# Shifted-token layers on one Trainium2 core: who scales and shifts the feed-forward norm's tiles, VectorE or ScalarE

## What is computed

```python
def shift_tokens(t):
    a, s = jnp.split(t, 2, -1)
    s = jnp.pad(s, ((0, 0), (1, 0), (0, 0)))[:, :-1]
    return jnp.concatenate([a, s], -1)
def ffn_layer(x, g, bln, W1, b1, W2, b2):
    mu = x.mean(-1, keepdims=True)
    var = ((x - mu) ** 2).mean(-1, keepdims=True)
    xn = (x - mu) / jnp.sqrt(var + 1e-05) * g + bln
    hg = xn @ W1 + b1
    a, gate = jnp.split(hg, 2, -1)
    return a * jax.nn.gelu(gate, approximate=False) @ W2 + b2
for i in range(6):
    x = attn_layer(shift_tokens(x), Wqkv[i], q_scale[i], k_scale[i], Wo[i]) + x
    x = ffn_layer(shift_tokens(x), ln_g[i], ln_b[i], W1[i], b1[i], W2[i], b2[i]) + x
```

## Time and profile before

| what | value |
|---|---|
| median of 3 runs | 4652.31 us (4650.04 to 4658.37) |
| profiled execution, its own time | 4656.79 us |
| its span | 4655.0 us |
| PE busy | 4112.3 us (88%) |
| PE weight loads | 2362.1 us (51%) |
| DVE busy | 3561.9 us (77%) |
| ACT busy | 2988.6 us (64%) |
| POOL busy | 2212.4 us (48%) |
| granted TensorE clock, mean | 0.935 |

### The profile page before, as it was taken

The page is one execution under the profiler, slowest core; times in us unless marked ns, Lnnn a source line. Parts: engine busy times, 40 slices in busy tenths (PEclk is TensorE's granted clock), DMA queues, the critical chain, the costliest instruction groups (busy, mean ns, idle before and its releaser), DMA issues. The chain is left out here.

```text
span 4655.0 us, 112822 instructions
## 1 busy us (share of the span) xinstructions
PE 4112.3 (88%) x40172; PEld 2362.1 (51%) x40175; DVE 3561.9 (77%) x8496; ACT 2988.6 (64%) x5496; POOL 2212.4 (48%) x1392
## 2 busy tenths in 40 slices
PE   8969999999999999999999999999999953747635
PEld 5644555555555555555555555555555532635533
DVE  7878888888888888888888888888888846356441
ACT  3427777777777777777777777777777745645302
POOL 0006665665656656566566656656565500140006
PEclk9989999999999999999999999999999975868557
DMA  1013222322223222232222322223222200000202
GB/s 41 1 54 67 62 58 62 80 59 61 60 60 81 63 59 60 58 82 65 59 59 60 76 65 63 57 64 75 64 60 61 58 17 12 1 1 6 82 9 35
DMA packets 187828, 246.44 MB, mean 53 GB/s; under 512 B 88677, under 2 KB 129383, under 8 KB 187367
## 3 DMA queue, kind: packets, MB, share of 16 engines
q1 hardware_dynamic: 182054, 240.47, 22.2%
q0 software_dynamic: 5632, 4.33, 0.7%
HBM read 41.65 MB, written 14.30 MB: 12 GB/s over the span
## 5 line engine op out<-in xcount | busy, mean ns | idle before, releaser
L1234 POOL TENSOR_TENSOR f_rot_a<-f_rot_a,f_norm 128x1024 f32<-128x1024 f32 x384 | 730.4, 1902 | 996.1 <-DVE f_norm L1073 963.6
L1226 POOL TENSOR_TENSOR f_rot_a<-f_rot_a,f_rot_b 128x1024 f32<-128x1024 f32 x384 | 908.5, 2366 | 246.3 <-issue 213.6
L832 PE MATMUL f_bank<-f_w_vo,f_xs_t 128*64 128x512 f32 x3072 | 828.5, 617 | 24.5 <-ACT f_vo L1303 24.5
L1303 ACT ACTIVATE f_vo<-f_bank 128x512 f32<-128x512 f32 x768 | 457.0, 595 | 395.9 <-PE f_bank L832 385.9
L1294 ACT ACTIVATE f_squares<-f_bank 128x512 f32<-128x512 f32 x768 | 456.4, 594 | 295.5 <-PE f_bank L819 215.6
L1052 DVE TENSOR_TENSOR f_rot_a<-f_bank,f_rot 128x512 f32<-128x512 f32 x768 | 525.0, 684 | 83.4 <-DVE f_stat L1101 42.3
L1055 DVE TENSOR_TENSOR f_rot_b<-f_bank,f_rot 128x512 f32<-128x512 f32 x768 | 516.8, 673 | 0.0
L864 PEld LDWEIGHTS f_bank<-f_k_t,f_q_t 128*32 128x32 f32 x12288 | 313.6, 109 | 315.4 <-issue 162.4
L1059 DVE TENSOR_REDUCE f_sums<-f_squares 128x16 f32<-128x1024 f32 x384 | 464.9, 1211 | 1.6
L1315 ACT ACTIVATE f_k_t<-f_bank 64x512 f32<-64x512 f32 x768 | 449.2, 585 | 4.8 <-PE f_bank L854 0.3
L1240 POOL TENSOR_TENSOR f_prob<-f_score,f_stat 128x512 f32<-128x512 f32 x384 | 400.4, 1043 | 98.6 <-DVE f_stat L1105 98.6
(11 more groups left out here) (445 smaller groups left out, 7235.4 us busy)
## 6 DMA issues: line engine op xcount, KB each, us to landing
f_vo_off<-f_vo SPq DMA_DIRECT2D x1152, 128.0 KB, 2.3
f_vo_off<-f_vo SPq DMA_DIRECT2D x384, 64.0 KB, 2.0
f_w_qk<-in_Wqk SPq DMA_DIRECT2D x12, 512.0 KB, 5.9
f_vo_dram<-f_vo_pair SPq DMA_DIRECT2D x48, 128.0 KB, 1.8
f_x_shifted<-s_all SPq DMA_DIRECT2D x48, 128.0 KB
f_x_shifted<-s_all SPq DMA_DIRECT2D x48, 127.0 KB
f_w_vo<-f_vo_dram SPq DMA_DIRECT2D x10, 512.0 KB, 4.0
e_w<-in_e_W SPq DMA_DIRECT2D x2, 2048.0 KB, 12.1
```

The lines of the kernel that those rows point to most:

```text
L832: done = nc.tensor.matmul(bank[V][64 * n:64 * n + 64, :], x, w_vo[:, 4 * g:4 * g + 4, n, :], start=True, stop=True)
L1226: nc.gpsimd.tensor_tensor(rot_a[:, slot, :, :], rot_a[:, slot, :, :], rot_b[:, g, :, :], ALU.add).then_inc(rot_summed, 1)
L1234: nc.gpsimd.tensor_tensor(heads, heads, over(norm[:, 16 * g:16 * g + 16], [128, 16, HEAD_DIM]), ALU.mult).then_inc(qk_normed, 1)
L1303: nc.scalar.activation(vo[:, g, 2 * (t % 2) + j, :], flat(V), ACT.Copy).then_inc((va_copied, vb_copied)[j], 1)
```

## The change: what it does

VectorE no longer writes the normalised tiles. In its place in round 1 it makes one instruction, four columns `-mean * inverse deviation` (`offsets`), and signals `f_measured`. ScalarE then makes the four tiles as `x * scale + bias` with the Identity function, in two pairs: tiles 0 and 1 between the square of q's first half and `copy_k` of the first half, tiles 2 and 3 between the square of k's second half and `copy_q` of the second half. `f_normed` comes from the last of the four. Nothing is changed on PE, POOL and SP.

```diff
+        f_offset = sb("f_offset", [128, PASS_TILES])
...
-            def normalise(p):
+            def offsets(p):
                 if live(p + 2, 0):
                     dve.wait_ge(norms_made, count(p + 2, 1))
                 else:
                     chain.wait()
                 if has(p, 1):
-                    dve.wait_ge(f_turned, p)
-                for t in range(PASS_TILES):
-                    last = nc.vector.tensor_scalar(f_n[:, 128 * t:128 * t + 128], x_shifted[:, t, :], f_mv[:, t, 0:1], norm[:, 32 + t:33 + t], ALU.subtract, ALU.mult)
-                    if t < PASS_TILES - 1:
-                        chain.mark(last)
-                last.then_inc(f_normed, 1)
+                    dve.wait_ge(f_normed, p + 1)
+                nc.vector.scalar_tensor_tensor(f_offset[:, :], f_mv[:, :, 0], -1.0, norm[:, 32:32 + PASS_TILES], ALU.mult, ALU.mult).then_inc(f_measured, 1)
...
                     if r == 1 and has(p, 2):
-                        normalise(p - 2)
+                        offsets(p - 2)
...
+            def normalise(p, half):
+                act.wait_ge(f_measured, p + 1)
+                if half == 0 and has(p, 1):
+                    act.wait_ge(f_turned, p)
+                for t in (2 * half, 2 * half + 1):
+                    last = nc.scalar.activation(f_n[:, 128 * t:128 * t + 128], x_shifted[:, t, :], ACT.Identity, bias=f_offset[:, t:t + 1], scale=norm[:, 32 + t:33 + t])
+                if half == 1:
+                    last.then_inc(f_normed, 1)
...
                     if on(r):
                         square(p, r, 0, 0)
+                    if r == 1 and has(p, 2):
+                        normalise(p - 2, 0)
                     if on(r - 1):
                         copy_k(p, r - 1, 0)
                         seed(p, r - 1, 0)
                         copy_values(p, r - 1, 1, 1)
                     if on(r):
                         square(p, r, 1, 1)
+                    if r == 1 and has(p, 2):
+                        normalise(p - 2, 1)
```

More of the change, by code:

```diff
@@ L575, in shifted_layers @@
         f_gate, gate_in, f_gelu, f_up = sem("f_gate"), sem("gate_in"), sem("f_gelu"), sem("f_up")
-        f_hidden, f_done, x_stored = sem("f_hidden"), sem("f_done"), sem("x_stored")
+        f_hidden, f_done, x_stored, f_measured = sem("f_hidden"), sem("f_done"), sem("x_stored"), sem("f_measured")
         ctx.callback(clear, nc, used)
```

## The result

The changed kernel takes 4688.65 us (median of 4 runs, 4685.7 to 4693.1) against 4653.63 us of the kernel before on the same chip: ratio 1.0075 [1.0058, 1.0093]. It is slower by 35.0 us where 34.5 were forecast. The profiled execution took 4685.7 us by its own time, with a span of 4683.9 us. The lines of the changed file are not those of the file before: `scores` is L865 (before L864), the turned norm L911 (L910), the turn of k L855 (L854), the projection of k L820 (L819), ACT's square L1292 (L1294), `copy_k` L1313 (L1315), `seed` L1319 (L1321), DVE's rotation L1053 (L1052), `length` L1060 (L1059), `store` L1145 (L1147). The columns are L1132, the Identity instructions L1341.

The account below looks back on a forecast made before the run. PE was taken to bound the kernel, with ACT lacking slack before `scores`. 46 passes x 0.77 = 35.4 us, less 0.9, gave +34.5 and 4687 us (+0.74%); own range 4676 to 4695, 8-in-10 range 4651 to 4702.

Parts of the forecast that it names:

- What bounds the kernel: PE, busy 976.4 of 1000 us; in round 1 ACT has at most 0.23 us of slack before `scores`.
- 1, the relief of DVE: Round 1: DVE gains 3.1 us a pass but then waits for ACT's square of k; worth 0.
- The estimate that DVE's busy time falls by 150 us: Expected sign in the profile after: DVE busy some 150 us less, ACT 92 us more.
- 2, the first pair: Two Identity instructions on ACT before `copy_k` in round 1 delay PE by 0.77 us a pass.
- The estimate that stands beside the sum: Skill page's formula for ACT's small tiles: 0.29 us each, 0.59 the pair, 27 us over 46 passes.
- 3, the second pair: Two Identity instructions between the square of k and `copy_q` fill 0.77 of ACT's 0.83 us idle time; cost 0.
- 4, the waits: ACT's wait for `f_measured` costs 0: DVE signals three us before ACT comes; later signals cost nothing either.
- 5, the ends: Tail norms taken at 0, at most 0.6 us each; pass 2 loses PE's 0.91 us wait for DVE once.
- The sum: 46 live passes x 0.77 = 35.4 us, less 0.9: +34.5 us.
- DVE was the bound: Faster: round 1's wait for the store closes, 0.33 us a pass, giving 4636 us; chance 0.14.
- Both partly: No change: half the pair hides, 0.38 us paid, and the store wait closes, -0.33; 4654 us; chance 0.12.
- ACT becomes the bound in more places: Slower still: a pair takes 1.05 us with a wait in front of each, 4700 us; chance 0.09.

Follow-up runs that it names:

- e4: Kernel before, norm still on DVE, plus two spare Identity instructions on ACT in front of `copy_k` in round 1, waiting for nothing: ratio 1.0070.
- e1: Changed kernel with all four Identity instructions behind ACT's square of k, none in front of `copy_k`: ratio 0.9997 against the kernel before.
- e3: Kernel before without the four normalising instructions on any engine; DVE makes only the columns and signals with them: ratio 0.9994.
- e9: Changed kernel with all four Identity instructions behind ACT's exponential and the columns made on DVE at the end of round 0: 0.9998 against the kernel before.
- e2: Changed kernel with three Identity instructions in front of `copy_k` and one behind ACT's square of k: ratio 1.0113 against the kernel before.
- e5: Changed kernel with columns first in DVE's round 1 and all four Identity instructions right after ACT's exponential: ratio 1.0025 against the kernel before.
- e7: Kernel before with only the store of pass p-3 moved on DVE to right behind the four normalising instructions: ratio 0.9960.

## Why the prediction was right, point by point

- **What bounds the kernel.** Right. PE is the bound at 97.6%, and ACT has no slack in front of `seed`: shown by e4, where two spare instructions there cost 0.70%, and e1, where their absence costs nothing.
- **1, the relief of DVE, taken at 0.** Right: e3 and e9. The price of the columns inside this step, 0.16 us, was wrong by a factor of ten: 1.73 us measured. It did no harm in passes 3 to 47, because even so they end at 2052.31, 1.3 us before ACT asks for them at 2053.63. In pass 2 it did (see 5). The estimate that DVE's busy time falls by 150 us failed by it: it fell by 3561.9 - 3490.4 = 71.5 us. ACT's rose by 3061.2 - 2988.6 = 72.6 us and not by 92, because instructions that overlap are counted once: 96 pairs x 0.77 = 74.
- **2, the first pair, 0.77 us on the path.** Right, and in the split foreseen: 0.69 at `scores`, the tenth of slack there lost again at L911 (0.09). Over the 44 intervals behind pass 3 the mean is 0.74. The third instruction of e2 confirms the price by itself. The spacing taken from the next block held: two take 0.87, so one starts 0.385 after the other. The estimate that stands beside the sum, 0.29 us for each and 27 us in all, was too low by a quarter.
- **3, the second pair, taken at 0.** Right. More: e1 shows that all four would fit there, since the turned norm's wait for the store covers what is late.
- **4, the waits, taken at 0.** Right for passes 3 to 47, by a margin of 1.3 us that e5, with another order, did not have.
- **5, the ends.** Incomplete. In pass 2 PE's wait of 0.91 us goes, as forecast, but a longer one comes. There is no down projection in that pass, so ACT comes to its first pair earlier by the 2.8 us that it takes elsewhere, ahead of the columns, and `scores` waits for it. The columns begin there at 479.89; at the forecast 0.16 us they would have been ready before ACT needed them (481.65 - 1.28 = 480.37), at 1.73 they are not:

```profile
481.65 0.88 ACT L1341 ACTIVATE f_f_n<-f_x_shifted,f_f_offset,f_norm 128x128 f32<-128x128 f32 x2 [1.28 <-DVE f_f_offset L1132]
```

```profile
484.24 1.08 PE L865 MATMUL f_bank<-f_k_t,f_q_t 128*32 128x128 f32 x32 [2.00 <-ACT f_bank L1319]
```

From the projection of k in front of `scores` to the turned norm, pass 2 takes 487.48 - 481.11 = 6.37 us against 485.63 - 480.19 = 5.44: 0.93 slower, where +0.77 - 0.91 = -0.14 was forecast. Right behind it a wait of 0.85 us goes that the forecast did not name, at the next `scores`, before and after:

```profile
489.10 1.08 PE L864 MATMUL f_bank<-f_k_t,f_q_t 128*32 128x128 f32 x32 [0.85 <-ACT f_bank L1321]
```

```profile
490.03 1.08 PE L865 MATMUL f_bank<-f_k_t,f_q_t 128*32 128x128 f32 x32
```

The delay against the kernel before falls there from 1.85 to 0.93 us, so the stretch from the norm of pass 2 to this point costs nothing in all, by two errors that cancel.

- **The sum.** +34.5 forecast, +35.0 measured. Some of the closeness is chance. From the first norm to the turned norm of pass 47 the profile has 34.3 - 0.92 = 33.4 us, 1.1 under the forecast: 0.74 a pass in place of 0.77. To these come the 0.92 us lost before the first norm, for which no cause is shown, and 0.9 us between pass 47 and the last turned norm in the tail (3790.55 - 3703.66 against 3755.32 - 3669.33). For the tail 0 was forecast, and e4, which has its norm on DVE, shows the same 0.9. That makes 35.2 us. Yet the profiled spans differ by only 28.9, since the blocks behind this one, which nobody changed, took some 6 us less in that execution. The interval of the ratio stands for +27 to +43 us.
- **The rival "DVE was the bound"** had a true part: the wait for the store is real, 0.33 us a pass. But what holds the store is its place in DVE's order behind ACT's square of k, not the amount of work on DVE: moving it wins the time (e7), relieving DVE does not (e3, e9).
- **The other two rivals** are answered by the timelines. "Both partly" needed a pair that hides by half and a store that comes early: of the 0.77 us 0.69 stand at `scores` and 0.09 at L911, which still waits for the store. "ACT becomes the bound in more places" needed 1.05 us for a pair and a wait in front of each: a pair takes 0.77 us from its start to the start of what follows, and in the pass shown ACT is not idle in front of either.

## What to carry to other kernels

Before work is moved from a busy engine to a less busy one, look at the row behind the place where it lands: an engine idle 26% of the time can have no slack at that place, and there each instruction costs its full length in every pass, while the same instructions a few places further down its list cost nothing. When the relieved engine's next instruction already coincides with the end of another engine's work, its relief only becomes a wait. And a wait that names an engine may be a matter of that engine's order: here moving one instruction up, with nothing offloaded, gave 0.4%.

## What the runs showed of the hardware

One DVE instruction of 128 x 4 took 0.15 us with POOL idle (e9), 0.91 (e5) and 1.73 us (changed kernel) beside POOL. The POOL rows of the changed kernel and of e5 show why:

```profile
2050.38 1.90 POOL L1232 TENSOR_TENSOR f_rot_a<-f_rot_a,f_norm 128x1024 f32<-128x1024 f32 x1 [0.17 <-POOL f_rot_a L1224]
```

```profile
2038.55 2.36 POOL L1224 TENSOR_TENSOR f_rot_a<-f_rot_a,f_rot_b 128x1024 f32<-128x1024 f32 x1 [0.40 <-issue]
```

POOL's instruction ends at 2052.28 and DVE's at 2052.31; in e5 at 2040.91 and 2040.93. So DVE's small instruction, whose two inputs lie in SBUF, is held until the running POOL instruction ends, while POOL's own takes its usual 1.90 us (1902 ns is the mean of all 384 of L1234 in the kernel before and of L1232 in the changed one). The Trainium skill ("SBUF — State Buffer", sections "Who interferes with whom" and "Summary: rules for kernel authors") says that a DVE instruction with two SBUF inputs contends with a GpSimd instruction that reads SBUF for a pair of ports, and that the second of the two to issue is blocked until the first finishes. The trace agrees: POOL starts first, at 2050.38 against 2050.58, and DVE ends 0.03 us behind it; the prediction took the price from a row with POOL idle and should have counted up to a whole POOL instruction.
